# Two 128-column weight products of a graph kernel's last layer, taken from one fp32 product each to three fp32r products each

## What is computed

```
x = layernorm(x + L0(x, adj, ...))    # adj @ x + x, weight, bias, row normalised
x = layernorm(x + L1(x, adj, ...))    # five gated recurrent steps
x = layernorm(x + L2(x, adj, ...))    # normalised adjacency, weight
x = layernorm(x + L3(x, adj, ...))    # the layer that the change touches
```

```
h0 = x @ W[0]
h1 = x @ W[1]
out = (A * M) @ h0 + (A * (1 - M)) @ h1 + bias
```

## Time and profile before

| | us |
|---|---|
| runs | 767.03, 765.65, 767.0 (median 767.0) |
| the profiled execution | 765.98 |
| its span, first to last instruction | 763.6 |
| TensorE busy | 748.1 |
| VectorE busy | 629.8 |
| ScalarE busy | 512.1 |
| GpSimd busy | 163.3 |

### The profile page before, as it was taken

One profiled execution on the slowest core, in us unless ns is written; L12 is line 12 of the kernel. 1 busy time (PEld: TensorE's weight loads), 2 busy tenths in 40 slices (PEclk: granted clock), 3 DMA queues, 4 the chain that ended last, 5 costly groups with the idle time before them and its releaser, 6 DMA issues.

```text
span 763.6 us, 11935 instructions
## 1 busy us (share of the span) xinstructions
PE 748.1 (98%) x3764; PEld 626.5 (82%) x3764; DVE 629.8 (82%) x1458; ACT 512.1 (67%) x1069; POOL 163.3 (21%) x309
## 2 busy tenths in 40 slices
PE   7999999999999999999999999999999999899996
PEld 6888788888888888888888888888887888788886
DVE  5899998888888998877777777887999999686654
ACT  4799877666666676666666666666587858874444
POOL 1778520000000000000000000000123257764343
PEclk9999999999999999999999999999999999999999
DMA  6500000000030001000000000000000000000112
GB/s 215 216 1 2 1 1 1 1 1 1 0 118 14 1 2 56 1 0 1 1 0 0 0 0 0 0 1 2 1 0 2 1 1 1 15 1 29 56 56 84
DMA packets 10566, 16.86 MB, mean 22 GB/s; under 512 B 3472, under 2 KB 5008, under 8 KB 9872
## 3 DMA queue, kind: packets, MB, share of 16 engines
q1 hardware_dynamic: 10512, 16.20, 6.2%
HBM read 8.85 MB, written 5.25 MB: 18 GB/s over the span
## 4 chain that ended last, share of the span: by engine, by line
PE 80%; DVE 8%; ACT 7%; issue 2%; POOL 2%; DMA 1%; SPq 0%; POOLq 0%; ACTq 0%; DVEq 0%
PE agg_ps L1053 12%; PE agg_ps L1055 12%; PE agg_ps L1054 12%; PE gate_ps L974 7%; PE gate_ps L976 6%; PE gate_ps L975 6%; PE cand_ps L974 4%; PE cand_ps L976 4%; PE cand_ps L975 4%; PE turn_ps L1092 4%; PE gate_ps L981 3%; PE cand_ps L981 2%; ACT res L441 2%; ACT feat L518 1%; PE turn_ps L1096 1%
## 5 line engine op out<-in xcount | busy, mean ns | idle before, releaser
L1053 PE MATMUL agg_ps<-adj_hi,nat_hi 128*128 128x512 f32 x384 | 152.2, 396 | 0.0
L1055 PE MATMUL agg_ps<-adj_hi,nat_lo 128*128 128x512 f32 x384 | 150.1, 391 | 0.0
L1054 PE MATMUL agg_ps<-adj_lo,nat_hi 128*128 128x512 f32 x384 | 149.6, 390 | 0.0
L649 POOL TENSOR_SCALAR shift<-mean_var 128x4 f32<-128x4 f32 x62 | 24.7, 399 | 424.1 <-DVE mean_var L874 421.8
L503 ACT ACTIVATE reset_hi<-gate_r 128x512 fp32r<-128x512 f32 x80 | 50.6, 633 | 82.7 <-DVE gate_r L841 82.7
L824 DVE TENSOR_TENSOR agg_lo<-agg_ps,agg_hi 128x512 fp32r<-128x512 f32 x80 | 55.2, 690 | 57.7 <-ACT agg_hi L470 57.7
L1055 PEld LDWEIGHTS agg_ps<-adj_hi,nat_lo 128*128 128x128 f32 x384 | 72.0, 188 | 16.3
L1054 PEld LDWEIGHTS agg_ps<-adj_lo,nat_hi 128*128 128x128 f32 x384 | 72.2, 188 | 15.5
L487 ACT ACTIVATE gate_r<-gate_ps,bias 128x512 f32<-128x512 f32 x80 | 55.2, 690 | 44.2 <-PE gate_ps L976 44.1
L1053 PEld LDWEIGHTS agg_ps<-adj_hi,nat_hi 128*128 128x128 f32 x384 | 72.1, 188 | 15.4 <-DVE adj_lo L898 0.3
L470 ACT ACTIVATE agg_hi<-agg_ps 128x512 fp32r<-128x512 f32 x80 | 48.7, 608 | 44.0 <-PE agg_ps L1055 43.7
(11 more groups left out here) (199 smaller groups left out, 1788.7 us busy)
## 6 DMA issues: line engine op xcount, KB each, us to landing
res<-in_x SPq DMA_DIRECT2D x16, 256.0 KB, 5.7
out<-res SPq DMA_DIRECT2D x16, 256.0 KB, 2.0
rows<-in_adj SPq DMA_DIRECT2D x4, 256.0 KB, 4.5
adj_hi<-eye_hi SPq DMA_DIRECT2D x1, 1024.0 KB, 9.9
adj_lo<-eye_lo SPq DMA_DIRECT2D x1, 1024.0 KB, 11.7
later<-in_adj SPq DMA_DIRECT2D x1, 1024.0 KB, 6.5
mix_rows<-mix SPq DMA_DIRECT2D x1, 1024.0 KB, 8.0
later<-mix_rows SPq DMA_DIRECT2D x1, 1024.0 KB, 4.8
```

What stands on the lines that cost most here:

```text
L1053: pe.matmul(ps, nat_hi[:, b, k, :], m_hi[:, k, :], start=(k == 0), stop=False)
L1054: pe.matmul(ps, nat_hi[:, b, k, :], m_lo[:, k, :], start=False, stop=False)
L1055: last = pe.matmul(ps, nat_lo[:, b, k, :], m_hi[:, k, :], start=False, stop=(k == T - 1))
```

## The change

For the L3 units alone, both weight products are made of split operands. The neighbourhood sum is copied by ACT to `agg_hi` instead of `agg_all`, and DVE subtracts to get `agg_lo`. `feat` of the unit is copied by ACT to `reset_hi` and subtracted by DVE to `reset_lo`, in the slot of the weight product. Both weights are split once, in slots 111 (ACT) and 112 (DVE). TensorE then does, for each block of 128 rows and each of the two operands, three fp32r products of 128 columns, and waits for the low parts. The order of the blocks and of the two halves of the last unit stays.

```diff
+LAST_PARTS_AT = MIX_AT + T - 1
 # ScalarE, slot(s), ahead of everything else in the slot
+                if s == LAST_PARTS_AT:
+                    act.wait_ge(z_done, AFTER - B)
+                    act.wait_ge(cand_done, AFTER - B)
+                    act.wait_ge(last_in, 32)
+                    for i, w in ((PART_REST, W_L3), (PART_SELF, W_SELF)):
+                        act.activation(w_hi[:, i, :], w_all[:, w, :], ACT.Copy).then_inc(last_hi_made, 1)
+                u = s - 1
+                if UNITS - B <= u < UNITS:
+                    act.wait_ge(turn_read, reads(TURN_NO["back", u - B]))
+                    act.wait_ge(gate_done, u)
+                    act.activation(reset_hi[:, :], feat[:, u % B, :], ACT.Copy).then_inc(self_hi_made, 1)
...
-                    act.activation((agg_hi if is_step(s) else agg_all)[:, s % 2, :], agg_ps[s % 2][:, :],
+                    act.activation((agg_hi if has_parts(s) else agg_all)[:, s % 2, :], agg_ps[s % 2][:, :],
 # VectorE, slot(s), ahead of line 731
+                u = s - 1
+                if UNITS - B <= u < UNITS:
+                    dve.wait_ge(self_hi_made, u - UNITS + B + 1)
+                    dve.tensor_tensor(reset_lo[:, :], feat[:, u % B, :], reset_hi[:, :].bitcast(F32),
+                                      ALU.subtract).then_inc(self_lo_made, 1)
 # VectorE, between the norm (line 821) and line 826
-                if is_step(s):
+                if s == LAST_PARTS_AT + 1:
+                    for i, w in ((PART_REST, W_L3), (PART_SELF, W_SELF)):
+                        dve.wait_ge(last_hi_made, i + 1)
+                        dve.tensor_tensor(w_lo[:, i, :], w_all[:, w, :], w_hi[:, i, :].bitcast(F32),
+                                          ALU.subtract).then_inc(last_lo_made, 1)
+                if s < UNITS and has_parts(s):
                     dve.wait_ge(agg_hi_made, ahead(s + 1))
+                    if stage(s) == L3:
+                        dve.wait_ge(gate_done, s - 1)
                     dve.tensor_tensor(agg_lo[:, s % 2, :], agg_ps[s % 2][:, :], agg_hi[:, s % 2, :].bitcast(F32),
                                       ALU.subtract).then_inc(agg_lo_made, 1)
 # TensorE
+            def by_rows_in_parts(ps, hi, lo, w, blocks, stop):
+                for t in blocks:
+                    at = ps[:, t * P:(t + 1) * P]
+                    cols = slice(t * P, (t + 1) * P)
+                    pe.matmul(at, hi[:, cols], w_hi[:, w, :], start=False, stop=False, skip_group_check=True)
+                    pe.matmul(at, hi[:, cols], w_lo[:, w, :], start=False, stop=False, skip_group_check=True)
+                    last = pe.matmul(at, lo[:, cols], w_hi[:, w, :], start=False, stop=stop, skip_group_check=True)
+                return last
...
-                if stage(u) == L3:
-                    pe.wait_ge(turn_read, reads(TURN_NO["back", u - B]))
-                    by_rows(ps, feat[:, u % B, :], W_SELF, False)
-                pe.wait_ge(agg_hi_made, u + 1)
-                by_rows(ps, agg_all[:, u % 2, :], w, True).then_inc(gate_done, 1)
+                halves = (ps, agg_ps[(u + 1) % 2]) if u == UNITS - 1 else (ps, ps)
+                pe.wait_ge(self_lo_made, u - UNITS + B + 1)
+                for half_ps, part in zip(halves, HALVES):
+                    by_rows_in_parts(half_ps, reset_hi, reset_lo, PART_SELF, range(part.start, part.stop), False)
+                pe.wait_ge(agg_lo_made, parted(u))
+                for h, (half_ps, part) in enumerate(zip(halves, HALVES)):
+                    last = by_rows_in_parts(half_ps, agg_hi[:, u % 2, :], agg_lo[:, u % 2, :], PART_REST,
+                                            range(part.start, part.stop), True)
...
 # TensorE, slot(s), ahead of the sum of unit s
                     if is_step(s - 2):
-                        pe.wait_ge(agg_lo_made, ahead(s - 2 - B + 1))
+                        pe.wait_ge(agg_lo_made, ahead(parted(s - 2)))
+                    elif stage(s - 2) == L3:
+                        pe.wait_ge(agg_lo_made, parted(s - 2))
```

More of the change, by code:

```diff
@@ L67, in is_inner, with has_parts, parted @@
     return B <= u < LAST
+def has_parts(u):
+    return is_step(u) or stage(u) == L3
+def parted(u):
+    return u - B + 1 if is_step(u) else u - 2 * B + 1
 def turn_lag(u):
@@ L223, in graph_layers @@
         W_L0, W_L2, W_L3, W_SELF = range(4)
+        PART_REST, PART_SELF = range(2)
         with ExitStack() as again:
@@ L313, in graph_layers @@
         rstd_made = sem("rstd_made")
+        last_hi_made, last_lo_made = sem("last_hi_made"), sem("last_lo_made")
+        self_hi_made, self_lo_made = sem("self_hi_made"), sem("self_lo_made")
         normed, normed_act = sem("normed"), sem("normed_act")
@@ L983, in by_rows @@
                 return last
+            def by_rows_in_parts(ps, hi, lo, w, blocks, stop):
[6 more added lines that the diff above has]
+                return last
             def layer(u):
                 ps = layer_ps[u % 4]
-                w = {L0: W_L0, L2: W_L2, L3: W_L3}[stage(u)]
+                w = W_L0 if stage(u) == L0 else W_L2
                 if u == 0:
@@ L993, in layer @@
                 if u == UNITS - B:
-                    pe.wait_ge(last_in, 32)
+                    pe.wait_ge(last_lo_made, 2)
                 if u < B:
@@ L999, in layer @@
                     pe.wait_ge(seeded, u - AFTER + 1)
-                if u == UNITS - 1:
-                    pe.wait_ge(turn_read, reads(TURN_NO["back", u - B]))
-                    halves = layer_ps[u % 4], agg_ps[(u + 1) % 2]
-                    for m, at in ((feat[:, B - 1, :], W_SELF), (agg_all[:, u % 2, :], W_L3)):
-                        if at == W_L3:
-                            pe.wait_ge(agg_hi_made, u + 1)
[L1007 to L1013, removed]
-                    return
-                if stage(u) == L3:
-                    pe.wait_ge(turn_read, reads(TURN_NO["back", u - B]))
-                    by_rows(ps, feat[:, u % B, :], W_SELF, False)
-                pe.wait_ge(agg_hi_made, u + 1)
-                by_rows(ps, agg_all[:, u % 2, :], w, True).then_inc(gate_done, 1)
+                if stage(u) != L3:
+                    pe.wait_ge(agg_hi_made, u + 1)
+                    by_rows(ps, agg_all[:, u % 2, :], w, True).then_inc(gate_done, 1)
+                    return
+                halves = (ps, agg_ps[(u + 1) % 2]) if u == UNITS - 1 else (ps, ps)
[6 more added lines that the diff above has]
+                                            range(part.start, part.stop), True)
+                    if u == UNITS - 1:
+                        last.then_inc((gate_done, half_done)[h], 1)
+                if u < UNITS - 1:
+                    last.then_inc(gate_done, 1)
             def candidate(u, ahead):
```

## The result

The changed kernel takes 782.92 us (median of 4 runs, 781.47 to 784.1) against 766.33 for the kernel before: 1.0207 times as long, 95% interval 1.0191 to 1.0223. The forecast was 783.

The account below looks back on a forecast made before the run. TensorE was taken to bound the kernel: 765.98 + 14.2 (passes) + 0.1 (transition) + 1.5 (end) = 781.8 us profiled, 782.8 on the runs' median, written 783. Forecast 780 to 786 (66%); range 778 to 804 (80%).

Parts of the forecast that it names:

- What bounds the stage: L3 stage: TensorE is busy throughout, so each nanosecond added there is one of the kernel until VectorE or ScalarE becomes late.
- The price of a new pass: L3 weight products: 111 ns per 128-column fp32r pass, about the load's pace; 24 passes cost 2.67 us a unit, not 1.78.
- my 14.2: Sixteen L3 units: +0.89 us each for 24 new passes instead of 16 old ones, +14.2 us in all.
- Copies, subtractions, weights: L3 slots: new ScalarE and VectorE work fits beside TensorE, VectorE 4.43 us a slot, 1.7 us slack for `reset_lo`.
- the transition: Slots 111 and 112, where the weights are split: 0.1 us added, bounds 0 and 0.9.
- The end: Unit 127: TensorE stalls 1.7 us for `reset_lo`; net +1.5 us with the earlier last root, bounds 1.2 and 2.0.
- earlier reciprocal root: Behind the last product: POOL is free sooner for the last root, which had begun about 0.2 us late.
- its lower end: Range's lower end, 778 us: 105 ns a pass and a cheap end, +11.8 + 1.2 on the median.
- 1: L3 products: narrow fp32r products run at the fp32 price, 223 ns each, giving 826 us; chance 12%.
- 3: L3 products: load and stream not overlapped at this width, 162 ns a pass, giving 802 us; chance 5%.
- 2: L3 products: loads taken in further ahead, pace the stream's 57 ns, 4.6 us slots, 762 us; chance 5%.
- 4: L3 slots: VectorE's list becomes the bound, adding 4 to 7 us, giving 787 to 790 us; chance 7%.

Follow-up runs that it names:

- e4: Changed kernel with all its new copies, subtractions and waits, but the old plain fp32 products on the high parts: 769.11 us, 1.0038 of the kernel before.
- a1: The changed kernel run again, unedited, as the measure for others on the same chip: median 783.69 us, 1.0203 of the kernel before.
- e1: Changed kernel with each of its 24 new products computing only the first 64 of 128 output columns: 785.74 us (2 runs).
- e2: Changed kernel with each of its 24 new products taking 256 moving columns, both weights side by side: 787.08 us (2 runs).
- e6: Changed kernel with six additional 512-column fp32r products ahead of unit 127's wait for `reset_lo`: median 784.04 us, 1.0192 of the kernel before.
- e5: Changed kernel with the parts of `feat` made one slot earlier into two alternating pairs of tiles: median 780.69 us, 1.0166 of the kernel before.

## Why the prediction was right

**What bounds the stage.** As told: TensorE, before and after, with its busy time equal to the slot in both. The slot grew by 0.86 us.

**The price of a new pass.** I took 0.111 us from the nearest rows; it is 0.11. The argument behind it, the load read from the first pass after an idle time (0.10 to 0.11 us), is the right one: at 64 columns the pace does not move, at 256 it moves by a hundredth, and with bf16 operands it halves. What I missed is the first of the 24, whose load hides behind the wide pass ahead of it (0.06 us). So a unit costs 2.63 us, not 2.67, and the fifteen that have a wide pass ahead of them 0.04 x 15 = 0.6 us less than my 14.2.

By the Trainium skill's rule (TensorE: Matmul & The Clock Gate, section "LDWEIGHTS") a load of 128 columns is 107 ns; the 0.11 us of this trace agrees for fp32r. For bf16 it doesn't hold here: passes every 0.056 us leave no room for a load of 107 ns. The 81 ns that its section "Back-to-back issue gap" gives for a sustained 128-column product did not come: fp32r took 0.11 us and bf16 0.056.

**Copies, subtractions, weights.** Hidden, as told: VectorE at 4.34 us a slot (forecast 4.43), no wait of TensorE in any slot but the last. The order of the lists left the slack that I worked out: in the slot from 716.26, `reset_lo` was done at 717.87 and TensorE came for it at 719.48, 1.6 us later (forecast 1.7). e4 hides the same work, in the same order, in slots of 4.99 us. At the transition TensorE waited only for `adj_lo`, as before, where I had put 0.1 us more.

**The end.** The stall was 1.77 us for a forecast 1.7. The 0.2 us that I took off for an earlier reciprocal root (POOL's `rstd`) weren't there. Before (first two lines; the root's is in the earlier trace rows) and after (the other four):

```profile
758.78 0.17 DVE L693 TENSOR_SCALAR mean_var<-mean_var 128x4 f32<-128x4 f32 x1
760.14 0.69 DVE L698 TENSOR_TENSOR res<-res,rstd 128x512 f32<-128x512 f32 x1 [0.41 <-POOL rstd L638]
...
773.10 0.41 PE L1031 MATMUL agg_ps<-w_hi,agg_lo 128*128 128x128 f32 x1
...
774.50 0.17 DVE L719 TENSOR_SCALAR mean_var<-mean_var 128x4 f32<-128x4 f32 x1
774.75 1.01 POOL L664 TENSOR_TENSOR rstd<-mean_var,half 128x4 f32<-128x4 f32 x1 [2.14 <-DVE mean_var L719]
775.86 0.69 DVE L724 TENSOR_TENSOR res<-res,rstd 128x512 f32<-128x512 f32 x1 [0.41 <-POOL rstd L664]
```

The root began 0.08 us behind the statistics it needs in both (758.95 to 759.03, 774.67 to 774.75), so POOL had not been late. From the last product's result (757.71 and 773.51) to the last elementwise step it was 2.43 us before and is 2.35 after. The fall of the clock, 0.7 us in the profile of after and 2.4 in a1's, was not in the sum.

**How close the sum came, and luck.** For the profiled execution the sum was 781.8 us, and 781.47 was measured (span 779.0). That is closer than its terms are, and in part luck. From the first L3 weight product to the end of the span, the kernel before takes 763.6 - 685.0 = 78.6 us and the changed one 779.0 - 684.3 = 94.7: 16.1 more, where I had 14.2 + 1.5 = 15.7. It is made of 13.6 for the passes, 1.8 for the stall and 0.7 for the clock, less 0.1 behind the last product: the clock, which I had left out, outweighs the pass that I missed. And the changed kernel reached this point 0.7 us earlier than the one before, 0.6 of which it had already gained 11 us into the program, where the two don't differ. One slip stands in the range: its lower end's own terms, 11.8 and 1.2 on the median of 767.0, give 780 and not 778; the measured 782.92 lies above both.

**Rivals.** 1 (fp32's price, 826 us) and 3 (load and stream one after the other, 802 us) fall with the pace; 2 (57 ns) does for fp32r, since the load is never taken in faster than one in 0.11 us, but it is just what bf16 does, and there the 4.6 us slot that I worked out for it came out at 4.55 without VectorE in the way. 4 falls with e4.

## What to carry to other kernels

Read the load of the stationary operand from the first pass after an idle time, where nothing covers it, and compare it with the stream of the moving one: in the products measured here the longer of the two is the pace (the transposes below are an exception). Narrow fp32r products are bound by the load, so splitting one fp32 product of 128 columns into three fp32r ones raises the number of loads from two to three and the time with it; bf16 parts load in half the time or less and made the same three products cheaper than the one, at a precision that wasn't measured. A step that is hidden behind the next unit's work in a loop is bare behind the last unit: price the end by itself, and make such parts one step early.

## What the runs showed of the hardware beyond the forecast

The first narrow fp32r pass behind a wide one costs its stream alone, 0.06 us at 128 columns and 0.03 at 64, since its load runs beside the wide pass.

TensorE's clock can be at 1.2 GHz for a few microseconds after 1.6 us of idle time, although TensorE is busy again, and how much of the work it catches differs between executions of the same program: 7 passes at half pace in one profile of the changed kernel, all 24 in the other. It also fell early in the kernel (0.71, 0.62 and 0.60 from 12 to 16 us in e1, e2 and e6, 1.00 in the others) and from 670 to 674 us (0.62, 0.57, 0.73 and 0.57 in e1, e2, e5 and e6). The first L3 weight product starts at 684.3 to 685.2 us in the profiles without either, at 686.3 with the second alone and at 687.8 to 688.3 with both: up to 4 us of a whole run, which is why small differences are better read from a stage than from single times.

The transposes stay unexplained: 0.11 us each, with a load of only some 55 ns. Something other than the load sets them; it was not tried.
